# Six opening loads of a MetaFormer block, put in another order

## The reference

```
x_n   = (x - mean over H) / sqrt(var over H + 1e-6)
x_dct = DCT over W, then over H, of x_n          # two products with 64x64 tables
low   = attention inside 8x8 blocks of x_dct     # q, k, v from Wq, Wk, Wv; softmax; projection
high  = gelu(1x1 conv) -> gelu(3x3 depthwise) + x_dct -> gelu(1x1 conv) + ...
x     = x + inverse DCT(coef*low + (1-coef)*high + x_dct)
```

```
logits  = t @ Wr + br ; the two largest give the weights
h       = gelu(layernorm(t) * ln_g + ln_b) @ W1 + b1)   # 64 -> 256, per expert
out     = t + sum over experts of gate * (h @ W2 + b2)  # 256 -> 64
```

## Time and profile before

| what | value |
|---|---|
| median of three runs | 230.36 us |
| profiled execution, its own time | 230.3 us |
| its span, first to last instruction | 228.4 us |
| PE matmuls busy | 205.6 us, 90% of the span |
| DVE, ACT, POOL busy | 126.7, 128.4, 46.9 us |
| granted TensorE clock, mean | 0.991 of full speed |
| SP issues: dct_h, x0, rest of c32, sm, x1, c16 | at 0.74, 1.17, 1.64, 2.11, 2.58, 3.06 us |

### The profile page before, as it was taken

The page is one execution under the profiler, slowest core; times in us unless marked ns, Lnnn a source line. Parts: engine busy times, 40 slices in busy tenths (PEclk is TensorE's granted clock), DMA queues, the critical chain, the costliest instruction groups (busy, mean ns, idle before and its releaser), DMA issues.

```text
span 228.4 us, 4925 instructions
## 1 busy us (share of the span) xinstructions
PE 205.6 (90%) x2096; PEld 112.0 (49%) x2096; DVE 126.7 (55%) x244; ACT 128.4 (56%) x207; POOL 46.9 (21%) x50
## 2 busy tenths in 40 slices
PE   7789788999967898978799699999999999999993
PEld 3565667565335587953424144444444444444430
DVE  0593145659959968999831534553334553335555
ACT  2257942035238542669684386666786666886640
POOL 5550492040079991030400000000000000000000
PEclk9999999999999999999799999999999999999999
DMA  6990000000000000000005953270804407053001
GB/s 219 289 265 15 0 3 6 3 0 7 0 0 4 0 3 0 3 0 0 3 1 148 225 128 76 59 174 0 182 4 110 119 4 184 0 136 96 0 0 47
DMA packets 6597, 14.36 MB, mean 63 GB/s; under 512 B 2736, under 2 KB 4144, under 8 KB 5680
## 3 DMA queue, kind: packets, MB, share of 16 engines
q1 hardware_dynamic: 6576, 14.06, 24.8%
HBM read 12.87 MB, written 1.18 MB: 62 GB/s over the span
## 4 chain that ended last, share of the span: by engine, by line
PE 62%; DVE 16%; ACT 6%; DMA 6%; POOL 5%; issue 2%; SPq 1%; POOLq 1%; DVEq 0%
PE psum L710 22%; PE psum L694 21%; PE psum L538 7%; DMA sm<-in_small 3%; DMA wide<-gate_store 3%; PE psum L512 2%; POOL place L920 2%; ACT place L747 2%; PE psum L548 2%; POOL place L919 1%; PE psum L557 1%; PE psum L498 1%; POOL place L918 1%; DVE st L1079 1%; DVE x L1071 1%
## 5 line engine op out<-in xcount | busy, mean ns | idle before, releaser
L694 PE MATMUL psum<-tok,w1s 128*64 128x512 f16 x512 | 61.1, 386 | 1.3 <-ACT hid L861 0.8
L1157 DVE SCALAR_TENSOR_TENSOR term<-psum,sm,wide 128x512 f32<-128x512 f32 x32 | 24.0, 751 | 62.5 <-PE psum L710 51.6
L861 ACT ACTIVATE hid<-psum,b1p 128x512 f32<-128x512 f32 x64 | 38.2, 702 | 16.7 <-PE psum L694 16.3
L694 PEld LDWEIGHTS psum<-tok,w1s 128*64 128x64 f16 x512 | 28.8, 111 | 36.2 <-issue 9.1
L861 ACT ACTIVATE w1f<-psum,b1p 128x512 f32<-128x512 f32 x32 | 19.6, 687 | 17.6 <-PE psum L694 17.5
L710 PE MATMUL psum<-hid,w 128*64 128x512 f32 x128 | 28.9, 593 | 0.0
L1162 DVE TENSOR_TENSOR x<-x,term 128x512 f32<-128x512 f32 x32 | 22.1, 692 | 1.1
L861 ACT ACTIVATE w1g<-psum,b1p 128x512 f32<-128x512 f32 x32 | 19.6, 714 | 0.3
L710 PE MATMUL psum<-w1g,w 128*64 128x512 f32 x64 | 15.1, 594 | 1.8 <-DVE term L1157 1.8
L710 PEld LDWEIGHTS psum<-hid,w 128*64 128x64 f32 x128 | 9.1, 137 | 15.1 <-issue 9.4
L538 PE MATMUL psum<-h_pad,tap_bd 64*64 64x512 f32 x144 | 15.9, 589 | 0.0
(11 more groups left out here) (139 smaller groups left out, 294.7 us busy)
## 6 DMA issues: line engine op xcount, KB each, us to landing
wide<-gate_store SPq DMA_DIRECT2D x14, 512.0 KB, 6.4
xs<-in_x SPq DMA_DIRECT2D x2, 512.0 KB, 5.7
w1f<-in_W SPq DMA_DIRECT2D x2, 512.0 KB, 10.0
block_out<-x SPq DMA_DIRECT2D x4, 256.0 KB, 6.2
wide<-gate_store SPq DMA_DIRECT2D x2, 384.0 KB, 5.4
c<-const SPq DMA_DIRECT2D x1, 548.5 KB, 4.6
hid<-in_W1T SPq DMA_DIRECT2D x1, 512.0 KB, 10.2
w<-in_W SPq DMA_DIRECT2D x1, 512.0 KB, 12.0
```

Of the source, the lines that this page charges most:

```text
L694: mm = pe.matmul(h_bank(n)[side * H:(side + 1) * H, :], w1s[:, part, e, k * P + side * H:k * P + (side + 1) * H], tok[:, pair, half, b, :] ...
L861: act.activation(hid_of[u % 4][:, t, :], h_bank(n), ACT.Gelu, bias=b1p[:, e * KT + k:e * KT + k + 1]).then_inc(gelu_ready, 1)
L1157: dve.scalar_tensor_tensor(term[:, u % 2, :], y_bank(u), b2t[:, e:e + 1], gate_b[part][:, e % (E // 2), :], ALU.add, ALU.mult).then_inc(te ...
```

## The change

The SP queue issues the opening loads in another order, and one of them is cut in two. The second transform's table (64 KB) gets a load and a semaphore (dct_w_in) of its own, directly behind x of pair 0. x of pair 1 follows it, then the small weights, and the other constants (484.5 KB) stand last of these. dct_over_w waits for dct_w_in in place of const_in, and windows, which needs ident, waits for const_in in addition.

```
-            sp.dma_start(c32[:, P:CONST_N], const32[:, P:CONST_N]).then_inc(const_in, 16)
+            sp.dma_start(c32[:, P:2 * P], const32[:, P:2 * P]).then_inc(dct_w_in, 16)
+            sp.dma_start(xs[:, 1, :], xv[1]).then_inc(x_in[1], 16)
             sp.dma_start(sm[:, :], small).then_inc(weights_in, 16)
-            sp.dma_start(xs[:, 1, :], xv[1]).then_inc(x_in[1], 16)
+            sp.dma_start(c32[:, 2 * P:CONST_N], const32[:, 2 * P:CONST_N]).then_inc(const_in, 16)
             sp.dma_start(c16[:, :], const16).then_inc(const16_in, 16)
...
             def dct_over_w(p):
-                pe.wait_ge(const_in, 16)
+                pe.wait_ge(dct_w_in, 16)
...
                 pe.wait_ge(dw_ready, 2 * (p + 1))
+                pe.wait_ge(const_in, 16)
                 for k2 in range(K):
```

More of the change, by code:

```diff
@@ L308, in metaformer @@
         x_in = [sem(f"x{p}_in") for p in range(PAIRS)]
-        dct_in = sem("dct_in")
+        dct_in, dct_w_in = sem("dct_in"), sem("dct_w_in")
         const_in, const16_in, weights_in = sem("const_in"), sem("const16_in"), sem("weights_in")
```

## The result

The changed kernel takes 233.73 us (median of six runs) against 230.17 us for the kernel before in the same set. The ratio is 1.0151, with a 95% interval from 1.0118 to 1.0184: it is slower by 1.5%, clear of noise, and outside the range of 229.7 to 232.0. The profiled execution took 233.6 us, its span is 231.7 us, so against the 230.3 us of the profiled execution before there are 3.3 us to find.

A forecast was written before the change was run, and what follows sets the result against it. The prediction took the opening chain of waits, started by the landing of sm, as the bound. To 230.3 us it added 0.35 for DVE steps beside POOL, giving 230.65, or 230.7 us, with a range of 229.7 to 232.0.

The forecast's parts named there:

- What opens the chain: Opening waits: the landing of sm releases coef_rest, DVE's first instruction, and the chain runs on into dct_over_w(0).
- The earlier table is worth nothing: Second transform's table lands just behind 4.8, but dct_over_w(0) does not start before 13.7, so no gain.
- this costs nothing: Extra load issue on SP, 0.42 us: free, since sm is issued long before its bytes have their turn.
- the landing of sm: Opening loads: 27.5 KB more issued up to and with sm, 0.13 us, so it lands at 8.3.
- My upper bound of 9.2: Latest landing of sm, if every load keeps the interval it showed and the table adds 0.3 us.
- the estimate of 0.8 us: From the skill's 0.95 us for a lone 64 KB load: the small table pushes sm back some 0.8 us.
- late weights: Rival, opening loads: sm lands at 9.2, L982 starts near 14.0, +1.1 us, 231.4 in all; chance 0.15.
- The gap on PE: PE idles from about 11.3 to 14 behind the router_weights matmul, before dct_over_w(0); near 2.7 us.
- the clock falls: Rival, PE behind its gap: the next stages run at 1.2 GHz, +1.2 on top of 0.35, 231.9; chance 0.13.
- DVE against POOL: Inverse square root of pair 0: eight DVE steps each last one POOL operation, L982 at 13.2, +0.35 us.
- What was hidden: POOL's weights 2.2 us later, conv_bd and taps covered by 7 and 5 us; pair 1 and late constants cost nothing.
- router_weights, which I cleared of blame: On PE it needs wr_bd from POOL at 10.9, just when dct_over_h(1) is ending, so no wait.

The follow-up runs named there:

- e3: Changed kernel with coef_rest and its wait for the small weights moved on DVE behind norm_columns(1); 229.46 us, ratio 0.9985 to the kernel before.
- e2: Changed kernel with the small weights loaded ahead of x of pair 1; 228.91 us, ratio 0.9957 to the kernel before.
- e1: Changed kernel with matmuls on zeros in PE's gap, six before router_weights and eleven behind; 232.31 us, ratio 1.0085 to the kernel before.
- e6: Kernel before, old load order, with only the constants split and the waits of the changed kernel; 232.93 us, ratio 1.0138.
- e8: The changed kernel run again, unaltered, in the set of e5 to e7; 232.35 us, ratio 1.0079 to the kernel before.
- e11: The changed kernel run again, unaltered, side by side with e12 on one chip; 233.35 us, ratio 1.0152 to the kernel before.
- e12: The kernel of e1 (changed kernel plus matmuls on zeros in PE's gap) run again beside e11; 231.63 us, ratio 1.0076 to the kernel before.
- e4: Kernel before, old load order, with coef_rest and its wait moved on DVE behind norm_columns(1); 229.62 us, ratio 0.9989.
- e5: Changed kernel without the small load: both transform tables in one first load of 128 KB; 231.75 us, ratio 1.0069 to the kernel before.
- e9: e5 plus matmuls on zeros in PE's gap, six before router_weights and five behind; 229.84 us, ratio 1.0016 to the kernel before.
- e7: Kernel before with only x of pair 1 and the small weights exchanged, no split of the constants; 233.44 us, ratio 1.0141.
- e10: Changed kernel with both tables in one load, small weights before x of pair 1, coef_rest later, router_weights behind windows(0); 229.18 us, ratio 0.9976 to the kernel before.

## Why the prediction was wrong

**What opens the chain: right.** sm's landing releases coef_rest, and everything up to dct_over_w(0) hangs on it. e3 shows it from one side, e2 from the other.

**"The earlier table is worth nothing", and of the extra issue "this costs nothing": wrong, the first cause.** The step that failed is the landing of sm, 8.3 by bytes. I counted the small load's 64 KB and one issue, and took it that the loads behind it would run on as before. They did not. x of pair 1, right behind the small load, was forecast at about 7 and landed at 8.2. In seven traces with the 64 KB load between x of pair 0 and the next large load, and 1531.5 or 1559 KB issued, sm lands at 9.76, 9.75 (e1), 8.5 (e3), 10.08 (e6), 9.92 (e8), 9.05 (e11) and 9.95 (e12); in four without it, at 8.17 (before), 7.4 (e4), 8.07 (e5) and 8.29 (e9). The means are 9.6 and 8.0, and the two groups do not overlap, but 8.5 and 8.29 are close. Bytes alone explain the second group (e5: 8.07 against 8.3 forecast) and e7. My upper bound of 9.2 was too low because its rows had no small load in the middle of the queue; it priced the load itself (0.3 us; the table landed at 4.6, right behind x of pair 0), when the price lay in what came behind it. The Trainium skill (DMA: Bandwidth & Descriptors, "Measured") has a duration for a 64 KB load by itself, and the estimate of 0.8 us that I made from it had the sign right; the traces show 1.6, and not in the small load but in its neighbours.

The price of "late weights" had a slip besides: by its own terms, 10.9 + 0.25 + 1.1 + 2.0, L982 comes at 14.25 and not near 14.0, so the rival stood for 231.7.

**The gap on PE: seen, its price about right, its chance wrong, the second cause.** The text had PE idle for 2.7 us and the measured idle time is 2.65, but the agreement is partly luck. The constants landed at 11.84 and not at 10.4, so router_weights came at 12.27 and not right behind dct_over_h(1), with another 1.66 us of idle time in front of it that the text did not have; and dct_over_w(0) was 1.3 us later than forecast. The rival "the clock falls" was priced at 1.2 us. The runs give 1.2 (e5 and e9), 1.6 (within the opening) and 1.7 us (between e11 and e12, after what the zeros cost). That the price was near is luck too: it came from the eight matmuls of the start, which took 3.60 us, and the profile has the granted clock at 1.00 from there on. I gave the case 0.13 because the clock had stayed up over 1.43 and 1.13 us of idle time and real matmuls stood on both sides. In the openings of all traces it fell behind longest idle stretches of 2.65, 2.63 (e11), 2.10 (e5), 4.14 (e6), 4.49 (e7) and 3.07 us (e8), and stayed up where the longest were 1.43 (before), 0.82 (e1), 1.00 (e2), 1.01 (e3), 1.66 (e4), 1.80 (e10), 1.18 (e9) and 1.61 us (e12). And I treated the rivals as exclusive. Late weights make the gap longer, so the first cause brings the second along; together they give 233.6, which no single case gave, and the range ended at 232.0.

**DVE against POOL: the mechanism right beside conv_bd, the term wrong.** Steps of the changed kernel, and POOL's first operations beside them:

```profile
12.06 0.17 DVE L965 TENSOR_TENSOR st<-st 128x16 f32<-128x16 f32 x1
12.27 0.18 DVE L966 SCALAR_TENSOR_TENSOR st<-st 128x16 f32<-128x16 f32 x1
12.48 0.32 DVE L964 SCALAR_TENSOR_TENSOR st<-st 128x16 f32<-128x16 f32 x1
12.84 0.34 DVE L965 TENSOR_TENSOR st<-st 128x16 f32<-128x16 f32 x1
13.21 0.33 DVE L966 SCALAR_TENSOR_TENSOR st<-st 128x16 f32<-128x16 f32 x1
```

```profile
11.91 0.22 POOL L878 TENSOR_TENSOR wr_bd<-sm,c 128x16 f32<-128x16 f32 x1 [8.41 <-DMA c<-const]
12.08 0.32 POOL L889 TENSOR_TENSOR enter_bd<-c,sm 128x64 f32<-128x64 f32 x1
12.36 1.15 POOL L884 TENSOR_TENSOR conv_bd<-c,sm 128x128 f32<-128x128 f32 x3
```

The starts are 0.21 apart, then 0.36 and 0.37, the length of one conv_bd operation. Beside conv_bd the trace agrees with the rule of the Trainium skill that the prediction took (SBUF — State Buffer, "Who interferes with whom"); beside wr_bd and enter_bd it does not show it, for there the steps keep 0.21. That is where the term failed. POOL came as far behind L981 (L979 before) as forecast, 0.48 us against 0.53, but the text gave the steps beside its first two operations 0.35 and 0.25. The 0.35 was the length of wr_bd in rows in which it lies beside coef_rest; here it takes 0.22. The eleven steps take 3.02 us, as long as before, and nothing is left of the 0.22 us by which this term was to lengthen them.

**What was hidden stayed hidden:** conv_bd, the taps, x of pair 1, the late constants. router_weights, which I cleared of blame, waited 1.66 us in the changed kernel, but DVE was later still.

**The account** in us, from one profile each: sm by bytes +0.1 (an estimate), small load +1.5, DVE against POOL 0, clock +1.6, together 3.2 of the 3.3. e9 is the test from the other side: with both causes out, the time is that of the kernel before.

## What to carry to other kernels

- A small load put between large ones can slow the loads behind it. Join it to another (here to the one at the head of the queue), and read the landing of the load that opens the chain, not of the one that was moved.
- Look at which wait stands first on each engine: one that nobody needs yet (coef_rest) turns a load order into a cost. And when a change widens a gap on PE, count the clock as part of the forecast, not as an accident.

## What the runs showed of the hardware that I had not expected

The rate of the loads from 4 to 6 us is lower with the 64 KB load in the queue: 265 and 238 GB/s (changed), 179 and 244 (e6), 170 and 198 (e8), against 411 and 350 (before), 372 and 335 (e7), 360 and 330 (e9). Over all fourteen traces the two stretches lie at 154 to 309 GB/s with it and at 309 to 414 without. The rate alone does not give the landing: e1 moved 298 and 304, e5 320 and 309, and sm landed at 9.75 and 8.07. Why what follows is slowed is not settled. No run parts the size of the load from its rows of 512 bytes, from its place behind x of pair 0, or from the mere fact that there is one load more; the one at the head of the queue, of the same shape, was in every kernel but three (e5, e9, e10).

Behind the opening the traces are not alike either. From keep_xd(0) to the last piece of the chain it is 200.0 us before and 200.1 in the changed kernel, but 199.6 in e8 and 200.9 in e9. The load of the gates is one reason (5.72 us in e8, 6.34 in e9), the later fall of the clock another: from 110 to 112 and from 114 to 116 us the granted clock is 0.85 and 0.79 before, and 0.50 in both stretches in e9. So one profile is no measure of a few tenths of a microsecond, and what makes the later fall longer is open.

A single small step can be held far longer than one POOL operation. In the changed kernel, for pair 1:

```profile
16.96 1.15 DVE L981 TENSOR_SCALAR st<-st 128x16 f32<-128x16 f32 x1
```

```profile
15.73 2.27 POOL L900 TENSOR_TENSOR tap_bd<-c,sm 128x64 f32<-128x64 f32 x9
```

Alone the step takes 0.17. Beside the nine tap_bd operations, 0.25 us each, it takes 1.15, and ends just behind the last of them (in e9 it takes 0.88, in e10 0.66). It reads one operand from SBUF, and so does the next, which starts the inverse square root; in the kernel before these two took 0.25 and 0.28 for pair 0, beside POOL, and 0.17 each for pair 1. dct_over_w(1) had slack enough for it here.
